# The softmax coefficient of a differential attention from two per-row scalars, with one inversion of the first sums per query block

## The chip, the cores and the metric

The kernel runs on one core of one Trainium2 chip. The metric is the device time in microseconds (us), from runs of the whole program; lower is better. The engines are named as in the profile: PE (matmul), PEld (PE's weight loads), DVE (vector), ACT (activation), POOL (the general vector engine), SP (the queue that issues DMAs).

## What is computed

The input is 8 sequences of 1024 rows of 512 numbers. Each row is normalised and projected to 32 query heads, 16 key heads and 8 value heads, the first two with rotary positions. Two neighbouring query heads make one output head, so there are 16 output heads. What matters here, cut from the reference:

```python
scores = jnp.einsum('bhqd,bhkd->bhqk', q, k)           # causal, 32 heads
probs = jax.nn.softmax(scores + causal, axis=-1)
probs = probs.reshape(bsz, H, 2, tgt_len, tgt_len)     # H = 16
diff = probs[:, :, 0] - lambda_full * probs[:, :, 1]
attn = jnp.einsum('bhqk,bhkd->bhqd', diff, v)
var = jnp.mean(attn ** 2, axis=-1, keepdims=True)
attn = attn * rsqrt(var + EPS) * subln_weight * (1 - LAMBDA_INIT)
out = attn @ Wo.T
```

Then follow the residual sum, a second normalisation, a feed-forward layer with ternary weights (512 to 2048 to 512, GELU) and a second residual sum.

## The kernel before

**Tiles and blocks.** A sequence is cut into 8 query blocks of 128 rows. Block t attends to 128 x (t + 1) keys, so its score rows are 128 to 1024 wide. The 8 blocks of sequence 0 are written out once, the 8 blocks of sequences 1 to 7 are the body of a loop, and three more blocks empty the pipeline. There are 64 blocks with 16 output heads each: 1024 heads in all.

**Steps of a block.** Each engine has its own program, written out by hand over 32 half steps (`hs`), two for a head. The order on an engine is fixed; semaphores tie the engines together. For one head:

1. PE writes two score tiles to PSUM (L832, and the mask by L833).
2. DVE takes the negated row maxima, `NM` (L665, one of two instructions, for blocks 4 to 7; L673, one instruction for both, for blocks 0 to 3).
3. ACT takes the exponentials, E1 and E2 (L541). Its accumulator writes the two row sums to `SUM[:, block parity, 0 or 1, head column]`.
4. DVE, in `diff`: the reciprocal of both sums into `RS` (L684, two elements a row), then `CC = SUM0 * neglam * (1 / SUM1)` (L686, one element a row), then `E1 = E2 * CC + E1` (L689, the full width). With SUM0 = first sum, E1 is then the difference of the two softmaxes times SUM0. `neglam` is minus the reference's `lambda_full`, one value for each row.
5. PE transposes E1 (L844), ACT copies the result out of PSUM (L553), and PE multiplies it with V (L867).

**The rest of a block.** The missing factor 1 / SUM0 is applied to all 16 heads at once, a block later at half step 6 (`AT_ROWS`, L727), from `RS[:, block parity, 0, :]`. The constant `SUM_INVERSE` (half step 5) stands in the schedule and is used by no line of the kernel before. Around the heads, DVE also does the normalisation (L623 to L631), the rotary products (L646 to L648), the remainders of split numbers (L660), the mean squares (L732, L735), and the sums with the residual (L738, L755). POOL does `x ** -0.5` (L437, L484), sums and splits (L442 to L449), the split of the hidden layer in three instructions (L458, L460, L462, in odd blocks only), and parts of the block's end (L481, L488, L500).

**Waits within `diff`.** L686 waits on semaphore `d_chain` for L684, and L689 waits on it for L686. L684 waits for both exponentials.

Of the kernel before, what the change touches and what calls it, by code (L numbers as in the profile page):

```python
# [32 lines left out]
F32 = mybir.dt.float32  # L33
# [3 lines left out]
ALU = mybir.AluOpType  # L37
# [3 lines left out]
P = 128  # L41
B, S, D = 8, 1024, 512
H, KVH = 16, 8
# [136 lines left out]
def diff_attention_ffn(nc, x, wqT, wkT, wvT, woT, lams, subw, w1T, b1, w2T, b2, rope, out):  # L180
    ctx = ExitStack()
    with ctx:
        def sb(name, shape, dt):
            return ctx.enter_context(nc.sbuf_tensor(name, shape, dt))

        def sem(name):
            return ctx.enter_context(nc.semaphore(name))
# [27 lines left out]
        DT = sb("DT", [P, TILES, HALF, P], F32)  # L215
        NM = sb("NM", [P, 8], F32)
        SUM = sb("SUM", [P, 2, 2, H], F32)
        RS = sb("RS", [P, 2, 2, H], F32)
        CC = sb("CC", [P, 2], F32)

        VST = sb("VST", [P, DKV], F32)
# [70 lines left out]
        max_ready = sem("max_ready")  # L292
        exp_done = sem("exp_done")
        d_chain = sem("d_chain")
        d_ready = sem("d_ready")
        t_ready = sem("t_ready")
        dt_ready = sem("dt_ready")
# [43 lines left out]
        def after(eng, signal, value):  # L341

            if not isinstance(value, int) or value > 0:
                eng.wait_ge(signal, value)
# [268 lines left out]
        def _(dve):  # L613
# [62 lines left out]
            def diff(b, i, n):  # L676

                u = i * H + n
                gu = b * N_U + u
                w = P * (i + 1)  # L680
                e = 512 * (u % 2) if i < 4 else 0
                col = 8 * (n // 8) + 4 * (n % 2) + (n % 8) // 2
                after(dve, exp_done, 2 * gu + 2)
                nc.vector.reciprocal(RS[:, i % 2, :, col], SUM[:, i % 2, :, col]).then_inc(d_chain, 1)  # L684
                after(dve, d_chain, 2 * gu + 1)
                nc.vector.scalar_tensor_tensor(out=CC[:, u % 2:u % 2 + 1], in0=SUM[:, i % 2, 0, col:col + 1], scalar=neglam[:, 0:1],  # L686
                                               in1=RS[:, i % 2, 1, col:col + 1], op0=ALU.mult, op1=ALU.mult).then_inc(d_chain, 1)
                after(dve, d_chain, 2 * gu + 2)
                nc.vector.scalar_tensor_tensor(out=E1[:, u % 2, 0:w], in0=E2[:, e:e + w], scalar=CC[:, u % 2:u % 2 + 1],  # L689
                                               in1=E1[:, u % 2, 0:w], op0=ALU.mult, op1=ALU.add).then_inc(d_ready, 1)  # L690

            def dve_work(T):
                b, t, nb, nf = T.b, T.t, T.nb, T.nf
                for hs in range(HS_TILE):
                    s, h = divmod(hs, 2)
                    if T.attend:
                        if t >= 4:
                            row_max(b, t, s, h)
                        elif h == 0:
                            row_max_pair(b, t, s)  # L700
                    if h == 0 and T.before(s - 1):
                        diff(*T.before(s - 1))
                    if T.attend:
                        slot = X[:, (t + 1) % 4, :]
                        if hs == LN1_STATS:

                            after(dve, x_in[(t + 1) % 2], 16 * (b * (TILES // 2) + (t + 1) // 2) + 16)
                            variance(0, slot, nb)
                        if hs == LN1_ROWS:
                            after(dve, m_x2t, nf)  # L710
                            normalise(0, slot, nb, xn_ready)
                        if hs == Q_ROPE:
                            rope_mul(nb, T.next, 0)
                        if hs == KV_ROPE:
                            rope_mul(nb, T.next, 1, b + 1)
                        if hs == Q_REST:
                            rest(nb, 0)
                        if hs == K_REST:
                            rest(nb, 1)
                    if T.finish:  # L720
                        tok = TOK[:, :].rearrange("p (c d) -> p c d", d=DV)
                        x1 = X1[:, (t - 1) % 4, :]
                        if hs == AT_ROWS:
                            after(dve, m_at, nf + 1)
                            if T.attend:
                                after(dve, m_xt, nb + 1)
                            nc.vector.tensor_tensor(tok, M[:, :].rearrange("p (c d) -> p c d", d=DV),  # L727
                                                    RS[:, (t - 1) % 2, 0, :].unsqueeze(2).broadcast_to([P, H, DV]),
                                                    ALU.mult).then_inc(attn_ready, 1)
                        if hs == MEAN_SQ:  # L730
                            after(dve, sq_ready, nf + 1)
                            nc.vector.tensor_reduce(MS[:, :], SQ[:, :].rearrange("p (c d) -> p c d", d=DV), AX.X,  # L732
                                                    ALU.add).then_inc(ms_chain, 1)
                            after(dve, ms_chain, nf + 1)
                            nc.vector.tensor_scalar(VE[:, :], MS[:, :], 1.0 / DV, EPS, ALU.mult, ALU.add).then_inc(ms_ready, 1)  # L735
                        if hs == O_SUM:
                            after(dve, m_wo, nf + 1)
                            nc.vector.tensor_tensor(x1, M[:, :], X[:, (t - 1) % 4, :], ALU.add).then_inc(x1_ready, 1)  # L738
                        if hs == LN2_STATS:
                            after(dve, x1_ready, nf + 1)  # L740
                            variance(1, x1, nf)
                        if hs == LN2_ROWS:
                            after(dve, m_ant, nf + 1)
                            normalise(1, x1, nf, xn2_ready)
                        if hs == LN2_REST:
                            after(dve, x2h_ready, nf + 1)
                            c = slice(P * ((t - 1) % 2), P * ((t - 1) % 2) + P)
                            nc.vector.scalar_tensor_tensor(
                                out=X2L[:, :, c], in0=M[:, :].rearrange("p (k n) -> p k n", k=KD), scalar=XS,
                                in1=X2H[:, :, c], op0=ALU.mult, op1=ALU.subtract).then_inc(x2_ready, 1)  # L750
                    if T.w2 and hs in OUT_AT:
                        j = OUT_AT.index(hs)
                        after(dve, f2_ready, T.no + j + 1)
                        after(dve, o_out, 16 * (T.no + j))
                        nc.vector.scalar_tensor_tensor(out=OUT[:, :], in0=F[:, :], scalar=1.0 / HS,  # L755
                                                       in1=X1[:, (t + j) % 4, :], op0=ALU.mult,
                                                       op1=ALU.add).then_inc(o_sum, 1)
# [277 lines left out]
```

## Time and profile before

| | |
|---|---|
| Time, median of 3 runs | 4437.56 us |
| Lowest and highest of the 3 | 4431.58 and 4438.31 us |
| Span of the profiled execution | 4427.3 us |
| The profiled execution's own time | not recorded; the median is 10.3 us above its span |
| Busy: PE, DVE, ACT, POOL | 81%, 78%, 66%, 33% of the span |
| Granted PE clock, mean of the core | 0.903 of full speed |

The span goes from the first to the last instruction of one execution; what lies around it is start and end of the program. Busy time of an engine is the union of its instructions' times. The idle time before an instruction is put down to what released it last.

### The profile page before, as it was taken

To read this page: it belongs to the slowest core of one execution; us is meant where nothing else is said; L and a number is where in the kernel's file an instruction comes from. 1 tells how busy PE (TensorE), PEld (TensorE's weight loads), DVE (VectorE), ACT (ScalarE), POOL (GpSimd) and SP (SyncE) were. 2 spreads that over 40 slices of the span, in tenths; PEclk is the share of its full clock that TensorE was granted. 3 is DMA by queue.
4 is the path that set the end of the run, shared out by engine and by line. 5 is a ranking of instruction groups with operands and counts; after the bars stand their busy time and mean duration, and the time that the engine had idled before them with its cause. 6 is when DMAs were issued, how large, how long until landed. Compare 5 with 4: busy or idle time off the path is not lost.

```text
span 4427.3 us, 80970 instructions
## 1 busy us (share of the span) xinstructions
PE 3604.6 (81%) x23454; PEld 2143.3 (48%) x23454; DVE 3467.0 (78%) x6124; ACT 2909.6 (66%) x6786; POOL 1450.2 (33%) x1563
## 2 busy tenths in 40 slices
PE   2688888888788887888878988888878888888886
PEld 1345544455444554544544544455544555444553
DVE  6778877888678886788867887678877788678891
ACT  1567756677566775667756766567666677567772
POOL 0233233332333333323343323433133332333323
PEclk7789989999899899998899988999989899899898
DMA  4212112211122112112122120222112121222110
GB/s 131 51 24 43 24 43 43 38 24 30 38 43 43 22 34 48 37 32 38 25 43 43 30 37 20 44 41 43 24 41 43 24 40 24 43 43 41 21 37 14
DMA packets 146768, 166.71 MB, mean 38 GB/s; under 512 B 16640, under 2 KB 117632, under 8 KB 145792
## 3 DMA queue, kind: packets, MB, share of 16 engines
q1 hardware_dynamic: 146304, 161.13, 18.0%
q8 instruction: 218, 3.57, 0.4%
q14 instruction: 246, 2.02, 0.2%
HBM read 105.95 MB, written 55.12 MB: 36 GB/s over the span
## 4 chain that ended last, share of the span: by engine, by line
PE 35%; DVE 28%; issue 22%; ACT 8%; DMA 3%; SPq 2%; POOL 2%; DVEq 1%; ACTq 0%; POOLq 0%
DVE NM L665 10%; PE M L867 6%; PE M L817 6%; PE F L889 5%; PE SP_ L832 5%; PE DP L844 5%; DVE E L689 4%; DVE CC L686 3%; PE F L902 3%; ACT E L541 2%; DMA KST<-scratch 2%; PE M L811 2%; ACT L541 2%; DVE RS L684 1%; DVE NM L673 1%
## 5 line engine op out<-in xcount | busy, mean ns | idle before, releaser
L541 ACT ACTIVATE E<-SP_,NM 128x256 f32<-128x256 f32 (+7 forms) x2048 | 1518.6, 743 | 733.6 <-DVE NM L665 526.4
L665 DVE TENSOR_REDUCE NM<-SP_ 128x1 f32<-128x896 f32 (+3 forms) x1024 | 1032.6, 1017 | 225.1 <-PE SP_ L833 222.9
L832 PE MATMUL SP_<-KST,QST 96*128 96x512 bf16 (+3 forms) x3072 | 864.1, 355 | 407.7 <-ACT E L541 345.5
L689 DVE SCALAR_TENSOR_TENSOR E<-E,CC 128x512 f32<-128x512 f32 (+7 forms) x1024 | 994.6, 971 | 36.1
L553 ACT ACTIVATE DT<-DP 128x512 f32<-128x512 f32 (+3 forms) x1024 | 527.8, 515 | 546.2 <-PE DP L844 524.0
L844 PE MATMUL DP<-ident,E 128*128 128x128 f32 x3328 | 614.5, 302 | 208.6 <-DVE E L689 207.3
L673 DVE TENSOR_REDUCE NM<-SP_ 128x2 f32<-128x1024 f32 (+3 forms) x512 | 419.8, 820 | 297.2 <-PE SP_ L833 290.3
L832 PEld LDWEIGHTS SP_<-KST,QST 96*128 96x128 bf16 x3072 | 278.7, 103 | 762.7 <-ACT E L541 537.1
L844 PEld LDWEIGHTS DP<-ident,E 128*128 128x128 f32 x3328 | 391.1, 153 | 382.2 <-issue 203.1
L889 PE MATMUL F<-X2H,W1Q 128*128 128x256 f16 x2048 | 502.0, 283 | 69.9 <-ACT HP L596 65.8
L817 PE MATMUL M<-WQKV,WT 128*128 128x512 f32 x1040 | 530.8, 607 | 8.4 <-DVE T L648 4.1
L889 PE MATMUL F<-X2L,W1Q 128*128 128x256 f16 x2048 | 501.1, 283 | 0.0
L833 PE MATMUL SP_<-maskb,identb 128*128 128x128 bf16 x2048 | 460.9, 234 | 0.0
L902 PE MATMUL F<-W2Q,HH 128*128 128x512 fp8e4 x1024 | 394.6, 385 | 33.1 <-DVE SQ L755 18.7
L541 ACT ACTIVATION_READ_ACCUMULATOR E<-SP_,NM 128x1 f32 x2048 | 414.3, 202 | 0.0
L902 PE MATMUL F<-W2Q,HL 128*128 128x512 fp8e4 x1024 | 393.0, 384 | 0.0
L686 DVE SCALAR_TENSOR_TENSOR CC<-SUM,neglam,RS 128x1 f32<-128x1 f32 x1024 | 317.9, 310 | 36.4
L458 POOL TENSOR_SCALAR HH<-HP 128x512 f16<-128x512 f32 x256 | 170.4, 666 | 529.9 <-ACT HP L602 513.7
L867 PE MATMUL M<-DT,V 128*32 128x256 f32 x4608 | 326.8, 422 | 0.1
L833 PEld LDWEIGHTS SP_<-maskb,identb 128*128 128x128 bf16 x2048 | 215.5, 105 | 192.1 <-issue 64.2
L462 POOL TENSOR_TENSOR HL<-HP,HH 128x512 f16<-128x512 f32 x256 | 297.9, 1164 | 21.3
L889 PEld LDWEIGHTS F<-X2H,W1Q 128*128 128x128 fp8e4 x2048 | 207.7, 101 | 171.9 <-issue 145.9
(86 smaller groups left out, 4780.3 us busy)
## 6 DMA issues: line engine op xcount, KB each, us to landing
QST<-scratch SPq DMA_DIRECT2D x390, 128.0 KB, 4.4
scratch<-SPL SPq DMA_DIRECT2D x65, 576.0 KB, 2.8
KST<-scratch SPq DMA_DIRECT2D x390, 64.0 KB, 5.0
X<-in_x SPq DMA_DIRECT2D x66, 256.0 KB, 3.1
out<-SQ SPq DMA_DIRECT2D x64, 256.0 KB, 2.1
KST<-in_w1T SPq DMA_DIRECT2D x1, 4096.0 KB, 19.2
DT<-in_w2T SPq DMA_DIRECT2D x1, 4096.0 KB, 28.7
WQKV<-in_wqT SPq DMA_DIRECT2D x1, 1024.0 KB, 7.3
```

Of the source, the lines that this page charges most:

```text
L541: act.activation(dst, score_out(i, 2 * n + k, w), ACT.Exp, bias=NM[:, (2 * u + k) % 8:(2 * u + k) % 8 + 1], scale=1.0, accum_out=SUM[:, i ...
L553: act.activation(DT[:, k0:k1, n % HALF, :], (DP, DX)[g][:, 0:P * (k1 - k0)].rearrange("p (k q) -> p k q", q=P), ACT.Copy).then_inc(dt_read ...
L665: nc.vector.tensor_reduce(NM[:, m:m + 1], score_out(i, 2 * n + k, P * (i + 1)), AX.X, ALU.max, negate=True).then_inc(max_ready, 1)
L673: nc.vector.tensor_reduce(NM[:, m:m + 2], SP_[:, k:k + 2, 0:P * (i + 1)], AX.X, ALU.max, negate=True).then_inc(max_ready, 2)
L689: nc.vector.scalar_tensor_tensor(out=E1[:, u % 2, 0:w], in0=E2[:, e:e + w], scalar=CC[:, u % 2:u % 2 + 1], in1=E1[:, u % 2, 0:w], op0=ALU. ...
L817: ins = pe.matmul(M[:, :], WT[:, P * j:P * (j + 1)], w[:, j, c0:c0 + 512], start=(j == 0), stop=(j == KD - 1))
L832: pe.matmul(SP_[:, k[a // 512], 0:n], q, KST[0:ROWS, a // P:(a + n) // P, kk, :], start=True, stop=not last)
L833: ins = pe.matmul(SP_[:, k[(w - P) // 512], (w - P) % 512:(w - P) % 512 + P], identb[:, :], maskb[:, :], start=False, stop=True)
L844: ins = pe.transpose((DP, DX)[g][:, P * (k % 4):P * (k % 4 + 1)], E1[:, u % 2, P * k:P * (k + 1)], ident[:, :])
L867: ins = pe.matmul(M[DV * q:DV * (q + 1), 0:2 * P], V[:, k, v:v + DV], DT[:, k, 2 * q:2 * q + 2, :], start=(k == 0), stop=(k == i), skip_gr ...
L889: ins = pe.matmul(F[:, 2 * P * j:2 * P * (j + 1)], W1Q[:, c, P * f:P * (f + 1)], xp[:, c, :], start=(c == 0 and xp is X2H), stop=(c == KD ...
L902: ins = pe.matmul(F[:, :], hp[:, f, P * j:P * (j + 1)], W2Q[:, f, :], start=(f == 0 and hp is HH), stop=(f == FT - 1 and hp is HL))
```

## The change

Three things are done. The reciprocal of a head takes the second sum alone, into a new tile `R2` of two columns (one for each head parity). The coefficient CC is made by a `tensor_scalar` with one tensor input (R2) and two scalar operands that are read per row from SBUF (the first sum and `neglam`), in place of a `scalar_tensor_tensor` with two tensor inputs (SUM and RS) and one such scalar. And the first sums of a block are inverted by one new reciprocal of 16 elements a row at half step 5 of the next block, into an `RS` that has one copy in place of two; L727's counterpart waits for it on a new semaphore, `inv_ready`.

```diff
-        RS = sb("RS", [P, 2, 2, H], F32)
+        R2 = sb("R2", [P, 2], F32)
+        RS = sb("RS", [P, H], F32)
...
                 after(dve, exp_done, 2 * gu + 2)
-                nc.vector.reciprocal(RS[:, i % 2, :, col], SUM[:, i % 2, :, col]).then_inc(d_chain, 1)
+                nc.vector.reciprocal(R2[:, u % 2:u % 2 + 1], SUM[:, i % 2, 1, col:col + 1]).then_inc(d_chain, 1)
                 after(dve, d_chain, 2 * gu + 1)
-                nc.vector.scalar_tensor_tensor(out=CC[:, u % 2:u % 2 + 1], in0=SUM[:, i % 2, 0, col:col + 1], scalar=neglam[:, 0:1],
-                                               in1=RS[:, i % 2, 1, col:col + 1], op0=ALU.mult, op1=ALU.mult).then_inc(d_chain, 1)
+                nc.vector.tensor_scalar(CC[:, u % 2:u % 2 + 1], R2[:, u % 2:u % 2 + 1], SUM[:, i % 2, 0, col:col + 1],
+                                        neglam[:, 0:1], ALU.mult, ALU.mult).then_inc(d_chain, 1)
...
+                        if hs == SUM_INVERSE:
+                            nc.vector.reciprocal(RS[:, :], SUM[:, (t - 1) % 2, 0, :]).then_inc(inv_ready, 1)
                         if hs == AT_ROWS:
+                            after(dve, inv_ready, nf + 1)
                             after(dve, m_at, nf + 1)
                             if T.attend:
                                 after(dve, m_xt, nb + 1)
                             nc.vector.tensor_tensor(tok, M[:, :].rearrange("p (c d) -> p c d", d=DV),
-                                                    RS[:, (t - 1) % 2, 0, :].unsqueeze(2).broadcast_to([P, H, DV]),
+                                                    RS[:, :].unsqueeze(2).broadcast_to([P, H, DV]),
                                                     ALU.mult).then_inc(attn_ready, 1)
```

DVE's instructions at half steps 4 to 6 of block 1, before (L673 to L689 are one head's; NM are the row maxima, E stands for E1 and E2, M is a PSUM tile):

```order
L631 TENSOR_SCALAR TOK<-X,MV,RST 128x512 [waits ln1_rstd]
L673 TENSOR_REDUCE NM<-SP_ 128x2 [waits s_ready]
L684 RECIPROCAL RS<-SUM 128x2 [waits exp_done]
L686 SCALAR_TENSOR_TENSOR CC<-SUM,neglam,RS 128x1 [waits d_chain]
L689 SCALAR_TENSOR_TENSOR E<-E,CC 128x256 [waits d_chain]
L673 TENSOR_REDUCE NM<-SP_ 128x2 [waits s_ready]
L684 RECIPROCAL RS<-SUM 128x2 [waits exp_done]
L686 SCALAR_TENSOR_TENSOR CC<-SUM,neglam,RS 128x1 [waits d_chain]
L689 SCALAR_TENSOR_TENSOR E<-E,CC 128x256 [waits d_chain]
L727 TENSOR_TENSOR TOK<-M,RS 128x512 [waits m_xt,m_at]
```

The same place in the changed program, where R is the new tile R2 and the line numbers are those of the changed kernel:

```order
L633 TENSOR_SCALAR TOK<-X,MV,RST 128x512 [waits ln1_rstd]
L675 TENSOR_REDUCE NM<-SP_ 128x2 [waits s_ready]
L686 RECIPROCAL R<-SUM 128x1 [waits exp_done]
L688 TENSOR_SCALAR CC<-R,SUM,neglam 128x1 [waits d_chain]
L691 SCALAR_TENSOR_TENSOR E<-E,CC 128x256 [waits d_chain]
L726 RECIPROCAL RS<-SUM 128x16
L675 TENSOR_REDUCE NM<-SP_ 128x2 [waits s_ready]
L686 RECIPROCAL R<-SUM 128x1 [waits exp_done]
L688 TENSOR_SCALAR CC<-R,SUM,neglam 128x1 [waits d_chain]
L691 SCALAR_TENSOR_TENSOR E<-E,CC 128x256 [waits d_chain]
L732 TENSOR_TENSOR TOK<-M,RS 128x512 [waits m_xt,m_at,inv_ready]
```

A head has as many DVE instructions as before, in the same places and with the same waits. One row is new in a block: the reciprocal of 16 elements, one head ahead of the instruction that reads it.

## Rows read from the trace of the kernel before

**Rows 1.** The page: busy shares, then the chain that ended last, by engine.
```profile
PE 3604.6 (81%) x23454; PEld 2143.3 (48%) x23454; DVE 3467.0 (78%) x6124; ACT 2909.6 (66%) x6786; POOL 1450.2 (33%) x1563
...
PE 35%; DVE 28%; issue 22%; ACT 8%; DMA 3%; SPq 2%; POOL 2%; DVEq 1%; ACTq 0%; POOLq 0%
```

**Rows 2.** Stages of one sequence (blocks 2, 5 and 7): each engine's busy time.
```profile
core 0: us, PE busy (x) PEld busy (x) DVE busy (x) ACT busy (x) POOL busy (x), PEclk, DMA share, GB/s
...
2314.90:2367.80 52.90, 46.34 (x275) 25.51 (x268) 42.30 (x89) 30.39 (x88) 13.42 (x13) 0.98 0.25 49
...
2495.90:2572.60 76.70, 64.28 (x443) 41.29 (x440) 63.17 (x103) 61.17 (x126) 33.04 (x35) 0.89 0.15 27
...
2648.60:2738.70 90.10, 72.19 (x510) 46.55 (x509) 75.80 (x101) 69.20 (x125) 31.46 (x35) 0.88 0.12 25
```

**Rows 3.** The chain over the whole span, summed by line.
```profile
by line: issue 21.5%; DVE NM L665 10.1%; PE M L867 6.4%; PE M L817 6.3%; PE F L889 5.4%; PE SP_ L832 5.1%; PE DP L844 4.8%; DVE E L689 4.1%; DVE CC L686 3.4%; PE F L902 3.3%; ACT E L541 2.5%; DMA KST<-scratch 2.0%; PE M L811 1.6%; ACT L541 
```

**Rows 4.** Groups of DVE by line: busy us, mean ns; idle before.
```profile
L686 DVE SCALAR_TENSOR_TENSOR CC<-SUM,neglam,RS 128x1 f32<-128x1 f32 x1024 | 317.9, 310 | 36.4
...
L784 DVE TENSOR_SCALAR HP<-KST,thr 128x2048 f32<-128x2048 f32 x4 | 5.1, 1286 | 0.1
...
L761 DVE TENSOR_SCALAR WQKV<-WQKV 128x2048 f32<-128x2048 f32 x1 | 1.2, 1227 | 13.4 <-DMA ropet<-in_rope 13.4
```

**Rows 5.** Single lines of DVE: duration in ns, least/median/longest, first and last start.
```profile
L686 DVE SCALAR_TENSOR_TENSOR CC<-SUM,neglam,RS x1024: 218/219/1102, 89.4 to 4333.3; 128x1 f32<-128x1 f32 x171
...
L684 DVE RECIPROCAL RS<-SUM x1024: 148/157/171, 89.2 to 4333.1; 128x2 f32<-128x2 f32 x171
...
L627 DVE TENSOR_SCALAR VE<-MV x129: 153/154/155, 15.6 to 4359.1; 128x1 f32<-128x1 f32 x129
...
L631 DVE TENSOR_SCALAR TOK<-X,MV,RST x129: 530/541/945, 16.5 to 4360.0; 128x512 f32<-128x512 f32 x129
...
L735 DVE TENSOR_SCALAR VE<-MS x64: 174/174/176, 141.8 to 4345.4; 128x16 f32<-128x16 f32 x64
...
L732 DVE TENSOR_REDUCE MS<-SQ x64: 673/677/685, 141.1 to 4344.6; 128x16 f32<-128x512 f32 x64
```

**Rows 6.** The instructions in order of time: POOL and DVE in block 5.
```profile
2553.86 0.62 POOL L458 TENSOR_SCALAR HH<-HP 128x512 f16<-128x512 f32 x1 [11.00 <-ACT HP L602]
2554.07 0.15 DVE L627 TENSOR_SCALAR VE<-MV 128x1 f32<-128x1 f32 x1
...
2557.83 0.16 DVE L684 RECIPROCAL RS<-SUM 128x2 f32<-128x2 f32 x1
2557.92 0.62 POOL L460 TENSOR_SCALAR HP<-HP 128x512 f32<-128x512 f32 x1 [0.19 <-POOL HH L458]
2558.02 0.52 DVE L686 SCALAR_TENSOR_TENSOR CC<-SUM,neglam,RS 128x1 f32<-128x1 f32 x1
2558.58 2.01 DVE L689 SCALAR_TENSOR_TENSOR E<-E,CC 128x768 f32<-128x768 f32 x1
2558.63 1.15 POOL L462 TENSOR_TENSOR HL<-HP,HH 128x512 f16<-128x512 f32 x1
```

**Rows 7.** The same view: first and last of 122 coefficients longer than 0.521 us.
```profile
101.88 0.93 DVE L686 SCALAR_TENSOR_TENSOR CC<-SUM,neglam,RS 128x1 f32<-128x1 f32 x1
...
4322.16 1.08 DVE L686 SCALAR_TENSOR_TENSOR CC<-SUM,neglam,RS 128x1 f32<-128x1 f32 x1
4323.27 1.72 DVE L689 SCALAR_TENSOR_TENSOR E<-E,CC 128x1024 f32<-128x1024 f32 x1
```

**Rows 8.** L689: the page's group, its durations (ns), and two undisturbed ones.
```profile
L689 DVE SCALAR_TENSOR_TENSOR E<-E,CC 128x512 f32<-128x512 f32 (+7 forms) x1024 | 994.6, 971 | 36.1
...
L689 DVE SCALAR_TENSOR_TENSOR E<-E,CC x1024: 350/885/2286, 89.6 to 4333.5; 128x256 f32<-128x256 f32 x22, 128x640 f32<-128x640 f32 x22, 128x1024 f32<-128x1024 f32 x22, 128x128 f32<-128x128 f32 x21
...
2005.29 1.02 DVE L689 SCALAR_TENSOR_TENSOR E<-E,CC 128x768 f32<-128x768 f32 x1
...
2648.88 1.28 DVE L689 SCALAR_TENSOR_TENSOR E<-E,CC 128x1024 f32<-128x1024 f32 x1
```

More of the change, by code:

```diff
@@ L294, in diff_attention_ffn @@
         d_chain = sem("d_chain")
+        inv_ready = sem("inv_ready")
         d_ready = sem("d_ready")
```

## The prediction

> **What bounds the kernel now.** I read the page first. PE is busy for 81% of the span and DVE for 78%; on the chain of work that ended last PE has 35%, DVE 28% and issue 22% [rows 1]. So no engine is the bound alone. By stages, a late block (5 or 7) has DVE busy for 63.2 of 76.7 and 75.8 of 90.1 us, while an early one (2) has 42.3 of 52.9 us [rows 2]. DVE has the least room in the late blocks, where PE waits for it as much as it for PE. Then the chain by line: the coefficient L686 holds 3.4% of 4427.3, which is 150 us [rows 3], out of the 317.9 us that it is busy at all [rows 4]. That is 0.47, and I take it as the share of time on this spot of DVE that the span feels.
>
> **What L686 costs, and why it is uneven.** Its mean is 310 ns [rows 4], its median 219, its longest 1102 [rows 5], for one element a row. If all took 219 ns they would make 224 us; the other 94 us is something else. The instructions in order of time show it [rows 6]: at 2558.02 the coefficient starts while POOL's L460 runs (2557.92 to 2558.54), and it ends as L460 ends, after 0.52 us. L689 starts at 2558.58, POOL's L462 at 2558.63, and L689 takes 2.01 us where the same width takes 1.02 undisturbed [rows 8]. One head has waited for POOL twice, once in each instruction that has two tensor inputs in SBUF. L684, with one input, never takes over 171 ns, and L627, a `tensor_scalar` of one element, takes 153 to 155 in all 129 cases [rows 5], also where it starts inside L458 [rows 6]. L631, a `tensor_scalar` of 512 elements, does reach 945 against a median of 541 [rows 5].
>
> Counted over all rows, 269 coefficients are longer than 225 ns, and 122 of them longer than 521 ns [rows 7]; those 122 hold 70 of the 94 us.
>
> **The changed coefficient, undisturbed.** The trace has no `tensor_scalar` of one element with two scalars read from SBUF. I build it. One without such scalars: 154 ns (L627) [rows 5]. One scalar costs 59 ns: L784, with one, takes 1286 ns for 2048 elements, L761, with none, 1227 [rows 4]. Two cost about 119: L761 gives (1227 - 154) / 2048 = 0.524 ns an element, so 512 elements make 268, and L631's 541 less 268 less 154 leaves 119 [rows 4, 5]. So 154 + 119 = 273 ns, 54 more than 219. Over 1024 heads this is **+55 us of DVE**. Bounds: 154 ns if the scalars' reading is hidden (-67 us), 273 from above, as both ways to price a scalar agree.
>
> **The reciprocals.** One element in place of two: the least and longest of L684 are 148 and 171 for two [rows 5], one element at the measured 0.524 ns is lost in that, so 0 (from -9 us, if all took 148, to 0). The block's new one, 16 elements, is not in the trace; the nearest row of 16 elements is L735 with 174 ns, the far bound L732, which reads 512 elements, with 677 [rows 5]. I take 174, since L684 lies so near to L627: 64 x 0.174 = **+11 us of DVE** (11 to 43). Behind it on DVE stand the row maximum and a whole head before L727's counterpart asks for it, over a microsecond of work, so `inv_ready` costs nothing, except in the one closing block, where its cover is gone and it costs at most that 0.2 us. No DMA and nothing on the queues of SP and POOL moves.
>
> Costs together: 66 us of DVE, times 0.47, **+31 us** on the span.
>
> **What the wait is worth.** My choice is that the new coefficient, having one tensor input and one element, does not wait, like L627. L689 still does. It would start 273 + 35 ns after the coefficient's start (35 is 36.4 us over 1024, the idle time before L686 [rows 4]; the same before L689 by its 36.1 [rows 8]). A wait shorter than 308 ns is then gone; of a longer one 308 ns is. That is 24 us for the 147 short ones and 122 x 0.308 = 38 us for the long, together 62.
>
> The second wait goes as well, where there was a first. L689 undisturbed takes 350 ns for 128 columns and 1.28 us for 1024 [rows 8], about 817 on the mean of the eight widths, 836 us in all; it is busy 994.6 [rows 8], so 158 us of it are waits. In the head of rows 6, L689 would wait at 2558.33 already, take over at 2558.54 when L460 ends, ahead of L462, and be through at 2559.56 in place of 2560.59. Counted over all rows, 62 of the 158 us stand right behind one of the 122 long coefficients, as the 1.72 at 4323.27 against 1.28 [rows 7, 8]; these I take as gone. Behind a shorter wait, 78 heads have a second one; there POOL's next instruction begins one coefficient (219 ns) earlier, which gives back 17 us. Together 62 + 62 + 17 = **141 us of DVE**.
>
> A saving on one path counts only until the next path is longest; a cost counts in full. PE, within 10% of DVE's load in every stage of rows 2, is that next path. So I weigh the saving with a third instead of 0.47: **-47 us**.
>
> The Trainium skill, page "SBUF — State Buffer", section "Who interferes with whom", has DVE and GpSimd share a port pair as an exclusive lock, taken by DVE instructions with two SBUF inputs and by those in a two-port mode, and it lists `tensor_scalar` among those that can enter such a mode. By the first half the coefficient stops waiting; by the second it could go on, and then the sum would be +31 instead of -16. For L631 the trace agrees with the second half (541 to 945 ns), for the one element of L627 it does not (153 to 155).
>
> **The sum.** Against the profiled execution: 4427.3 + 31 - 47 = 4411.3 us of span. What lies around it is 10.3 us, so 4421.6; against the median of the runs, 4437.56 - 16 = **4422 us**.
>
> **Rivals.**
>
> *A, the forecast: the first wait is gone and the second with it.* 4422 us, own range 4403 to 4440 (the saving weighed by 0.47: -66 + 31 = -35; by 0.2: -28 + 31 = +3). For it: L627 and L684 never wait, and each instruction of POOL in rows 6 is followed by a gap in which a waiting DVE can take over. Chance 0.5.
>
> *B, the wait is handed on.* L689 waits for what L686 waited for, and afterwards still collides with POOL's next instruction, as POOL, no longer held up by the coefficient, has that one ready sooner. Then only the 62 us go, a third of which is 21: 4437.56 + 31 - 21 = 4448. For it: POOL's three instructions follow each other within 0.2 us. Against: L686 itself was let in between two of them. Chance 0.2.
>
> *C, slower: the coefficient goes on waiting.* Reading the two scalars, or the instruction's mode, needs what POOL holds. Then nothing is gained: 4437.56 + 31 = 4469. For it: no row shows a small `tensor_scalar` with scalars from SBUF beside a busy POOL, and L631 waits. Against: L627. It decides if less than 93 of the 141 us of DVE come back, since 93 / 3 = 31. Chance 0.12.
>
> *D, much faster.* The scalars' reading is hidden (no 55 us), and the whole 141 us count by 0.47: -66 + 5 = -61, so 4377. Against: L784 and L631 show the price openly. Chance 0.08.
>
> *E, it does nothing that can be told.* Cost and saving both vanish in the waits for PE, of which DVE has many in blocks 0 to 3: 4437. Chance 0.1.
>
> **How the numbers follow.** The forecast is A's, 4422. A and B with their surroundings, E, and most of C are held by 4392 to 4466; below it lies D, above it a part of C, 2 in 10 with the tails. 0.2% of the time is 9 us, about what a measurement of this kernel can tell from no change. Faster than 4428.7: 0.35 from A, 0.08 from D, 0.02 from B and E, 0.45. Within: 0.13 of A, 0.08 of B, 0.08 of E, 0.01 of C, 0.30. Slower: 0.10 of B, 0.11 of C, the rest from the edges of A and E, 0.25.
>
> **What the changed kernel's profile would show.** The coefficient has a median near 273 ns and hardly a longer one, its busy time falls from 318 to about 280 us; a longest far above 300 ns would be C. L689's busy time falls from 995 us towards 950 (less 62 and 17, more the 32 us of long waits that it meets itself); under B it grows, by those 32 us. The block's reciprocal takes near 174 ns, 64 times; an amount per element of tens of ns would show there. The odd blocks, with 31 to 33 us of POOL's work, become shorter; the even ones, with 13 us in block 2 [rows 2], gain less and may be longer by at most 16 x 0.054 + 0.174 = 1.0 us each. The forecast is wrong if the two scalars cost more than 119 ns in a one-element instruction, if POOL wins the gap before L689, or if the blocks turn out to be set by PE, so that 141 us less of DVE's waits leave the span where it is.

## The result

The changed kernel takes 4372.64 us (median of 4 runs, 4370.70 to 4373.63), the kernel before 4437.94 us beside it. The ratio is 0.9853, 95% interval 0.9840 to 0.9867: 65 us, or 1.5%, faster. The forecast was 4422 us and its range ended at 4392, so the direction was right and the size too small by a factor of four.

The page of the changed kernel, busy shares and the chain, to stand beside [rows 1]:

```profile
PE 3625.1 (83%) x23454; PEld 2157.1 (49%) x23454; DVE 3369.0 (77%) x6188; ACT 2913.5 (67%) x6786; POOL 1495.9 (34%) x1563
...
PE 41%; DVE 25%; issue 19%; ACT 8%; DMA 3%; SPq 2%; POOL 1%; DVEq 1%; ACTq 1%; POOLq 0%
```

DVE is busy 98 us less (3467.0 to 3369.0), POOL 46 us more (1450.2 to 1495.9), and the span is 58.4 us shorter (4427.3 to 4368.9). These are numbers of one execution of each kernel. Every execution whose span is on record took 1.7 to 1.9 us longer than its span, so the profiled one of the kernel before took an estimated 4429.1 us. It was 8 us faster than the median, and the 10.3 us in the table ahead of the prediction are not start and end of the program. On the chain DVE has gone from 28% to 25%, PE from 35% to 41%. The same three blocks of the same sequence as in [rows 2]:

```profile
2275.80:2328.30 52.50, 46.59 (x271) 25.57 (x262) 41.88 (x89) 30.46 (x88) 13.76 (x14) 0.96 0.23 50
2456.50:2531.60 75.10, 63.64 (x452) 41.34 (x450) 61.94 (x103) 60.89 (x125) 33.54 (x35) 0.91 0.16 28
2609.70:2697.90 88.20, 72.85 (x507) 46.56 (x506) 71.26 (x102) 69.05 (x125) 34.07 (x35) 0.87 0.11 25
```

Against [rows 2] block 2 is 0.4 us shorter, block 5 is 1.6 us shorter and block 7 1.9 us. On the mean over the loop's sequences all odd blocks are shorter (by 0.8, 2.1, 1.3 and 1.9 us), but so is block 0, by 2.3 us, and block 6 is 2.0 us longer (76.1 to 78.1).

Now the lines that were changed, in groups (busy us, mean ns; idle before). Line numbers are 2 to 5 higher than before.

```profile
L688 DVE TENSOR_SCALAR CC<-R,SUM,neglam 128x1 f32<-128x1 f32 x1024 | 279.5, 273 | 37.3
...
L691 DVE SCALAR_TENSOR_TENSOR E<-E,CC 128x512 f32<-128x512 f32 (+7 forms) x1024 | 928.6, 907 | 36.2
...
L686 DVE RECIPROCAL R<-SUM 128x1 f32<-128x1 f32 x1024 | 158.7, 155 | 65.7 <-ACT E L543 61.1
...
L633 DVE TENSOR_SCALAR TOK<-X,MV,RST 128x512 f32<-128x512 f32 x129 | 74.3, 576 | 2.5 <-POOL RST L439 1.5
...
L726 DVE RECIPROCAL RS<-SUM 128x16 f32<-128x16 f32 x64 | 15.7, 245 | 0.0
```

and the coefficient's spread, least, median and longest:

```profile
L688 DVE TENSOR_SCALAR CC<-R,SUM,neglam x1024: 272/273/276, 89.4 to 4274.7; 128x1 f32<-128x1 f32 x171
```

No coefficient waits any more: 276 ns is the longest of 1024, where it was 1102 [rows 5]. Among them are 295 that start while a wide instruction of POOL (256 or 512 elements a row) has over 220 ns to run. Its undisturbed time is the 273 ns that the prediction had built from four other rows. The row sum (L689 before, L691 now) is busy 928.6 us in place of 994.6 [rows 8].

The head of [rows 6], in the same block of the same sequence:

```profile
2518.62 0.15 DVE L686 RECIPROCAL R<-SUM 128x1 f32<-128x1 f32 x1
2518.70 0.62 POOL L462 TENSOR_SCALAR HP<-HP 128x512 f32<-128x512 f32 x1 [0.19 <-POOL HH L460]
...
2518.81 0.27 DVE L688 TENSOR_SCALAR CC<-R,SUM,neglam 128x1 f32<-128x1 f32 x1
...
2519.12 1.02 DVE L691 SCALAR_TENSOR_TENSOR E<-E,CC 128x768 f32<-128x768 f32 x1
...
2519.41 1.74 POOL L464 TENSOR_TENSOR HL<-HP,HH 128x512 f16<-128x512 f32 x1
```

Before, the coefficient took 0.52 us and the row sum 2.01; now they take 0.27 and 1.02. From the reciprocal's start to the row sum's end it was 2.76 us and is 1.52. POOL's L464, 1.15 us long when undisturbed, takes 1.74: the row sum now comes first, and POOL waits for DVE instead of DVE for POOL. By line, POOL's additional busy time is 28 us in the first instruction of this split (L458 before, 170.4 us, now 198.2), 18 in its third (297.9, now 315.7) and 7 and 6 in two others, less 15 in its second (195.4, now 180.1).

The second wait can be counted. Before, 95 row sums start 10 to 47 ns ahead of an instruction of POOL and still wait for it, 62 us in all; that of [rows 6], 47 ns ahead, is one. In the changed kernel 3 do, 1.8 us. Row sums that start 49 to 200 ns ahead of POOL, 23 before and 10 now, do not wait.

### The profile page after: what moved, and what is told of

Its sections match the earlier page's. It is cut to its first block, busy times and chain, and to the rows that moved or that the text cites. A ratio compares the mean times of both kernels' runs of the same rounds, so it can differ in the third digit from the quotient of the medians.

```text
span 4368.9 us, 81035 instructions
## 1 busy us (share of the span) xinstructions
PE 3625.1 (83%) x23454; PEld 2157.1 (49%) x23454; DVE 3369.0 (77%) x6188; ACT 2913.5 (67%) x6786; POOL 1495.9 (34%) x1563
## 4 chain that ended last, share of the span: by engine, by line
PE 41%; DVE 25%; issue 19%; ACT 8%; DMA 3%; SPq 2%; POOL 1%; DVEq 1%; ACTq 1%; POOLq 0%
DVE NM L667 9%; PE M L822 7%; PE M L872 7%; PE SP_ L837 6%; PE F L894 6%; PE DP L849 5%; PE F L907 4%; DVE E L691 3%; ACT E L543 3%; DVE CC L688 2%; DMA KST<-scratch 2%; PE M L816 2%; DVE NM L675 2%; PE SP_ L838 1%; PE DX L849 1%
## 5 line engine op out<-in xcount | busy, mean ns | idle before, releaser
L691 DVE SCALAR_TENSOR_TENSOR E<-E,CC 128x512 f32<-128x512 f32 (+7 forms) x1024 | 928.6, 907 | 36.2
L894 PE MATMUL F<-X2H,W1Q 128*128 128x256 f16 x2048 | 512.1, 287 | 71.0 <-ACT HP L598 67.0
L894 PE MATMUL F<-X2L,W1Q 128*128 128x256 f16 x2048 | 510.7, 286 | 0.0
L460 POOL TENSOR_SCALAR HH<-HP 128x512 f16<-128x512 f32 x256 | 198.2, 774 | 519.9 <-ACT HP L604 503.7
L872 PE MATMUL M<-DT,V 128*32 128x256 f32 x4608 | 342.8, 439 | 0.1
L464 POOL TENSOR_TENSOR HL<-HP,HH 128x512 f16<-128x512 f32 x256 | 315.7, 1233 | 21.3
L688 DVE TENSOR_SCALAR CC<-R,SUM,neglam 128x1 f32<-128x1 f32 x1024 | 279.5, 273 | 37.3
```

The costliest lines, as they stand in the source:

```text
L872: ins = pe.matmul(M[DV * q:DV * (q + 1), 0:2 * P], V[:, k, v:v + DV], DT[:, k, 2 * q:2 * q + 2, :], start=(k == 0), stop=(k == i), skip_gr ...
L894: ins = pe.matmul(F[:, 2 * P * j:2 * P * (j + 1)], W1Q[:, c, P * f:P * (f + 1)], xp[:, c, :], start=(c == 0 and xp is X2H), stop=(c == KD ...
```

## The experiments

Each was timed beside the kernel before on the same chip, 4 to 11 runs each. To compare them with each other, their ratios to the kernel before are used, and 0.001 is 4.4 us. "Above the changed kernel" is the ratio less 0.9853, times 4438; with intervals of about 0.0013 on either side of each ratio, such a difference is known to within some 8 us. DVE's busy time is that of one profiled execution. The two theories at the start: that DVE's time counts by about 0.6 wherever it lies (58.4 / 98), against a rival by which other parts of the edit or other weights had their share.

**The coefficient's form alone.** Both sums are inverted in each head as before.

```diff
-                nc.vector.scalar_tensor_tensor(out=CC[:, u % 2:u % 2 + 1], in0=SUM[:, i % 2, 0, col:col + 1], scalar=neglam[:, 0:1],
-                                               in1=RS[:, i % 2, 1, col:col + 1], op0=ALU.mult, op1=ALU.mult).then_inc(d_chain, 1)
+                nc.vector.tensor_scalar(CC[:, u % 2:u % 2 + 1], RS[:, i % 2, 1, col:col + 1], SUM[:, i % 2, 0, col:col + 1],
+                                        neglam[:, 0:1], ALU.mult, ALU.mult).then_inc(d_chain, 1)
```

> The coefficient's new form alone; both sums are inverted per head as before and there is no block inversion. Theory 1 (all of the gain is the coefficient's wait, and DVE time counts by about 0.6 wherever it is): as the changed kernel without its 15.7 us of block inversion and with 4 us more of reciprocals, so 12 x 0.6 = 7 us below it: 4366 us. Rival (the block inversion and the shorter reciprocals brought part of it): above the changed kernel, 4380 us or more. In both the coefficient takes 273 ns and never waits.

Measured: 0.9856 (0.9841 to 0.9871), 4377.81 us. The whole gain is there without the block inversion. The time itself lies between the two that were expected, but the ratio is the changed kernel's. Of the 12 us of DVE to be saved against the changed kernel 8 are there (3361.1 against 3369.0 us), and they brought nothing that shows. The coefficient (279.4 us) and the row sum (927.7) are as short as in the changed kernel.

**The inversions alone.** The coefficient keeps two inputs.

```diff
+                nc.vector.scalar_tensor_tensor(out=CC[:, u % 2:u % 2 + 1], in0=SUM[:, i % 2, 0, col:col + 1], scalar=neglam[:, 0:1],
+                                               in1=R2[:, u % 2:u % 2 + 1], op0=ALU.mult, op1=ALU.mult).then_inc(d_chain, 1)
-                nc.vector.tensor_scalar(CC[:, u % 2:u % 2 + 1], R2[:, u % 2:u % 2 + 1], SUM[:, i % 2, 0, col:col + 1],
-                                        neglam[:, 0:1], ALU.mult, ALU.mult).then_inc(d_chain, 1)
```

> The block inversion and the one-element reciprocals alone; the coefficient keeps the two-input form. Theory 1: 12 us more of DVE than before, 7 us slower: 4445 us; the coefficient's mean stays near 310 ns. Rival (the inversion brought part of the gain): under 4430 us.

Measured: 0.9997 (0.9988 to 1.0006), 4437.63 us. They neither help nor cost; the 7 us of cost that theory 1 expected lie just outside the interval. The coefficient, with one-element reciprocals and all, waits as before, and the row sum behind it too:

```profile
L691 DVE SCALAR_TENSOR_TENSOR E<-E,CC 128x512 f32<-128x512 f32 (+7 forms) x1024 | 998.1, 975 | 36.1
...
L688 DVE SCALAR_TENSOR_TENSOR CC<-SUM,neglam,R 128x1 f32<-128x1 f32 x1024 | 316.8, 309 | 36.3
```

So the 38 us less in the coefficient and the 66 us less in the row sum both hang on the one changed instruction.

**One more instruction with one input in every head** of the changed kernel, which prices evenly spread DVE time.

```diff
                 after(dve, exp_done, 2 * gu + 2)
+                nc.vector.tensor_scalar(DUM[:, u % 2:u % 2 + 1], SUM[:, i % 2, 1, col:col + 1], 1.0, 0.0, ALU.mult, ALU.add)
                 nc.vector.reciprocal(R2[:, u % 2:u % 2 + 1], SUM[:, i % 2, 1, col:col + 1]).then_inc(d_chain, 1)
```

> The changed kernel with one more DVE instruction a head in front of the reciprocal: a tensor_scalar of one element with one input and constants, into a tile that nothing reads, with nothing waiting for it. Two such instructions without a wait between them start 70 ns apart in the setup (85.05 and 85.12 us), so it costs 72 us of DVE if it behaves so, 158 us if it holds the next one for its full 154 ns. Theory 1 (DVE time in a head counts by 0.6): 72 x 0.6 = 43, 4416 us. Rival (a cost counts by 0.3 at most, since PE is the next bound, and only the waits behind POOL are dear): under 4394 us.

Measured: 0.9897 (0.9882 to 0.9912), 4394.49 us. DVE is busy 3428.2 us, 59 more, and the time is 20 us above the changed kernel: 0.33 for each us, with the 8 us of uncertainty 0.2 to 0.5, and so below theory 1's weight.

**The same with two inputs in SBUF.**

```diff
+                nc.vector.tensor_tensor(DUM[:, u % 2:u % 2 + 1], SUM[:, i % 2, 0, col:col + 1], SUM[:, i % 2, 1, col:col + 1], ALU.mult)
```

> As the run with one more one-input instruction, but the extra one is a tensor_tensor of one element with two inputs in SBUF (160 ns in the trace of before, against 154). Its difference to that run is the price of waiting for POOL once more in a head, at no other change. Theory 1: 94 us of waits in the extra instruction and up to 66 us more in the row sum behind it, by 0.6: 55 to 95 us above the one-input run. Rival (the wait is handed on, the row sum would have waited anyway): within 15 us of the one-input run.

Measured: 1.0038 (1.0026 to 1.0051), 4455.31 us, 0.0141 or 63 us above the run with one input. The two instructions side by side, first the one with one input, then the one with two, and that one's least, median and longest duration:

```profile
L687 DVE TENSOR_SCALAR DUM<-SUM 128x1 f32<-128x1 f32 x1024 | 149.0, 145 | 67.7 <-ACT E L544 64.1
```
```profile
L687 DVE TENSOR_TENSOR DUM<-SUM 128x1 f32<-128x1 f32 x1024 | 280.2, 274 | 68.9 <-ACT E L544 66.0
```
```profile
L687 DVE TENSOR_TENSOR DUM<-SUM x1024: 142/158/1112, 88.4 to 4340.1; 128x1 f32<-128x1 f32 x171
```

A second input in SBUF costs 131 us: 14 ns more in the median (158 against 144), 14 us of it, and the rest waits. DVE is busy 117 us more (3544.9 less 3428.2). The time went up by 63 us: 0.54 for each us. The rival, that the row sum would have waited anyway, is refuted; it is only 11 us shorter (918.5 against 929.5 us). So waits look dearer than evenly spread work, though 0.54 and 0.33 are apart by hardly more than their uncertainty. Three theories for that were put on record: their place (P), their size in one head (S), or something of the waits themselves (L).

**A delay of one input in the 34 heads of a sequence that had waited before, and in 34 quiet ones.**

```diff
+AT_HEADS = {0: (3, 5, 7, 8, 10), 1: (3, 5, 7, 11, 13, 14, 15), 2: (5, 8), 3: (5, 7, 8, 9, 14, 15), 4: (5, 8, 10, 15), 5: (5, 8, 13), 6: (5, 8, 10), 7: (7, 8, 9, 13)}
...
+                if n in AT_HEADS[i]:
+                    nc.vector.tensor_reduce(DUM[:, u % 2:u % 2 + 1], ropet[:, :, :, :].rearrange("p a b c -> p (a b c)"), AX.X, ALU.max)
                 nc.vector.reciprocal(R2[:, u % 2:u % 2 + 1], SUM[:, i % 2, 1, col:col + 1]).then_inc(d_chain, 1)
```

> The changed kernel with one more DVE instruction, in 34 of the 128 heads of a sequence (272 in all): a maximum over 256 numbers of a table, one input, into a tile that nothing reads, in front of the reciprocal. The 34 are the heads whose coefficient waited for POOL in the trace of before. Such an instruction takes about 0.41 us and never waits for POOL, about 0.33 us from start to start, so some 90 us of DVE in all. Theory P (waits behind POOL are dear because of the heads in which they lie, where DVE holds up the span): it counts by 0.5 or more, 45 us above the changed kernel, 4418 us or more. Theory S (they are dear because each is large, and a small delay is taken up by slack): the same as the delay at quiet heads. Theory L (the waits themselves are special, as by what POOL loses; DVE time counts by 0.34 in every form): 31 us, 4403 us, in both.

> The same instruction as often in each block, but in 34 heads whose coefficient did not wait in the trace of before. Theory P: it counts by 0.34 or less, under 4403 us, and at least 15 us below the run with the delay at the waiting heads. Theory S: by 0.5, 4418 us, as that run. Theory L: 4403 us, as that run.

Measured: 0.9981 (0.9972 to 0.9990), 4430.05 us, at the heads that had waited, 57 us above the changed kernel; 0.9945 (0.9932 to 0.9959), 4415.31 us, at the quiet ones, 41 us above. DVE is busy 96 and 76 us more: 0.59 and 0.54. Theory L falls: DVE time of a kind that never waits for POOL is as dear as the waits when it comes in lumps. The place makes 16 us of difference, and 20 us of DVE busy time go with it, from row sums that wait more (942.6 against 919.7 us). Part of the 16 us may be the clock: PE's mean granted clock was 0.901 of full speed in the median run at the heads that had waited and 0.905 in that at the quiet ones.

**The form by head.** The two-scalar form only in the 34 heads, two inputs in the other 94.

```diff
+                if n in TWO_SCALARS[i]:
+                    nc.vector.tensor_scalar(CC[:, u % 2:u % 2 + 1], R2[:, u % 2:u % 2 + 1], SUM[:, i % 2, 0, col:col + 1],
+                                            neglam[:, 0:1], ALU.mult, ALU.mult).then_inc(d_chain, 1)
+                else:
+                    nc.vector.scalar_tensor_tensor(out=CC[:, u % 2:u % 2 + 1], in0=SUM[:, i % 2, 0, col:col + 1], scalar=neglam[:, 0:1],
+                                                   in1=R2[:, u % 2:u % 2 + 1], op0=ALU.mult, op1=ALU.mult).then_inc(d_chain, 1)
```

> The changed kernel, but the coefficient takes the two-scalar form only in those 34 heads of a sequence; the other 94 take the two-input form of before (219 ns in place of 273) with the one-element reciprocal. 752 x 54 ns = 41 us less of DVE. If uniform DVE time counts by 0.34 and the quiet heads stay quiet: 14 us below the changed kernel, 4359 us. If POOL's instructions move onto other heads, so that the two-input form waits in them: 4373 us or more.

Measured: 0.9864 (0.9848 to 0.9879), 4376.08 us, no better than the changed kernel. POOL's instructions did move onto heads that had been quiet: the two-input coefficient takes 238 ns on its mean in place of 219, and the row sum 918 against 907.

```profile
L695 DVE SCALAR_TENSOR_TENSOR CC<-SUM,neglam,R 128x1 f32<-128x1 f32 x752 | 178.8, 238 | 26.6
...
L692 DVE TENSOR_SCALAR CC<-R,SUM,neglam 128x1 f32<-128x1 f32 x272 | 74.2, 273 | 9.9
```

Of 41 us that were to be saved DVE kept 13.

**Two extra instructions with one input in every head.**

```diff
+                nc.vector.tensor_scalar(DUM[:, u % 2:u % 2 + 1], SUM[:, i % 2, 1, col:col + 1], 1.0, 0.0, ALU.mult, ALU.add)
+                nc.vector.tensor_scalar(DUM[:, 2 + u % 2:3 + u % 2], SUM[:, i % 2, 1, col:col + 1], 1.0, 0.0, ALU.mult, ALU.add)
```

> As the run with one more one-element instruction of one input per head, but with two of them: about 2 x 63 = 126 us more of DVE than the changed kernel, in equal parts on all heads. If its price is linear: 0.34 x 126 = 43 us, 4416 us. Theory S (small delays fall into slack, which runs out): more than twice the first one's 22 us, over 4425 us. If DVE's limit is rarely reached: under 4405 us.

Measured: 0.9996 (0.9979 to 1.0014), 4437.34 us, the median of 11 runs from 4415.29 us, at a granted clock of 0.915, to 4458.85, at 0.900. DVE is busy 137 us more and the time is 63 us above the changed kernel. The first such instruction cost 20 us, the second 44 for 78 us of DVE: 0.33, then 0.57. The price looks not linear, as theory S has it, though the second's extra cost, 24 us, has an uncertainty of some 16, but a price by the sum over all heads (theory C, put on record for the next two runs) would explain this too.

**The delay at half its size**, a maximum over 128 numbers, at quiet heads and at those that had waited.

```diff
-                    nc.vector.tensor_reduce(DUM[:, u % 2:u % 2 + 1], ropet[:, :, :, :].rearrange("p a b c -> p (a b c)"), AX.X, ALU.max)
+                    nc.vector.tensor_reduce(DUM[:, u % 2:u % 2 + 1], ropet[:, 0, :, :].rearrange("p b c -> p (b c)"), AX.X, ALU.max)
```

> The delay at the 34 quiet heads, but a maximum over 128 numbers in place of 256: about 0.20 us from start to start, 272 times, 54 us of DVE, which is less than the 65 us that one extra one-element instruction in every head adds (that cost 22 us). Theory S (a delay counts by its size in one head, as small ones fall into slack): 0.48 x 54 = 26 us above the changed kernel, 4399 us. Theory C (it counts by the sum over all heads; the first 65 us are cheap and the next dear, as the full delay of 90 us and the two extra instructions of 129 us suggest): 18 us or less, 4391 us or less.

> The same half delay at the 34 heads whose coefficient waited for POOL before: 54 us of DVE and, as in the full delay, some more waits of the row sum behind it. Theory C with the place counting too: 0.64 against 0.48 in the full delay, so a third more than at the quiet heads: 24 to 35 us above the changed kernel, 4397 to 4408 us. If the place counts only through size: as the quiet run within 5 us.

Measured: 0.9931 (0.9917 to 0.9945) and 0.9930 (0.9917 to 0.9944), 35 and 34 us above the changed kernel. The sum over the heads is less than that of the one extra instruction in each (DVE busy +54 and +43 us against +59), and the price is more (35 and 34 us against 20). The 15 us between the half delay at quiet heads and the one extra instruction have an uncertainty of 9. That speaks against theory C, which allowed 18 us at the quiet heads, and for S: a delay counts by how large it is in one head. The second run alone decides nothing, as C with the place counting too had said 24 to 35 us. A rival was not tested: the lumps also lie unevenly among the blocks, 7 heads in block 1 and 2 in block 2, and are made by another instruction. The place made no difference at this size. What may take up the small delays can be read in the idle time of the row maxima, in the changed kernel, with one extra instruction in each head, and with the half delay at quiet heads:

```profile
L667 DVE TENSOR_REDUCE NM<-SP_ 128x1 f32<-128x896 f32 (+3 forms) x1024 | 1034.2, 1018 | 257.8 <-PE SP_ L838 254.0
```
```profile
L668 DVE TENSOR_REDUCE NM<-SP_ 128x1 f32<-128x896 f32 (+3 forms) x1024 | 1032.6, 1018 | 226.2 <-PE SP_ L840 223.0
```
```profile
L671 DVE TENSOR_REDUCE NM<-SP_ 128x1 f32<-128x896 f32 (+3 forms) x1024 | 1032.9, 1017 | 244.2 <-PE SP_ L844 241.1
```

The 59 us that are spread evenly take 32 us out of DVE's idle time before the row maxima of blocks 4 to 7; the 54 us in lumps take 14. This is read from one execution of each. By these executions' own times alone (4370.70, 4398.84 and 4403.96 us) the weights are 0.48 and 0.62, and so nearer to each other than by the medians.

**The extra instruction on the kernel before.**

> The kernel before with the extra one-element instruction of one input in every head: 65 us more of DVE above where it stood, in the same form as the run on the changed kernel. If the price grows with DVE's load: 0.5 to 0.66 of 65, so 32 to 43 us above before, 4470 to 4481 us. If it levels off, as the changed kernel with two extra instructions (4437 us at 3506 us of DVE) suggests: under 4458 us.

Measured: 1.0067 (1.0054 to 1.0081), 30 us above before, for 65 us of DVE: 0.46. Neither branch was met cleanly; nothing shows that the price levels off.

**No reciprocal in the heads.**

```diff
-                nc.vector.reciprocal(R2[:, u % 2:u % 2 + 1], SUM[:, i % 2, 1, col:col + 1]).then_inc(d_chain, 1)
-                after(dve, d_chain, 2 * gu + 1)
-                nc.vector.tensor_scalar(CC[:, u % 2:u % 2 + 1], R2[:, u % 2:u % 2 + 1], SUM[:, i % 2, 0, col:col + 1],
+                nc.vector.tensor_scalar(CC[:, u % 2:u % 2 + 1], SUM[:, i % 2, 1, col:col + 1], SUM[:, i % 2, 0, col:col + 1],
...
-                after(dve, d_chain, 2 * gu + 2)
+                after(dve, d_chain, gu + 1)
```

> The changed kernel without the reciprocal of each head: the coefficient multiplies the second sum in place of its inverse, so the output is not the reference's. 158 us less of DVE busy, about 190 us less of its time. If PE is the bound by now (the version by head and the form alone, both with less DVE time than the changed kernel, were not faster): above 4355 us. If DVE time still counts by 0.34 or more: 65 us less or more, 4308 us or below.

Measured: 0.9675 (0.9661 to 0.9688), 4289.23 us, 79 us below the changed kernel, for 161 us less of DVE busy: 0.49. DVE is not off the path in the changed kernel; PE is not yet the bound alone. The granted clock was 0.919 against 0.900, and how much of the 79 us goes with it is not shown by this run.

| Run | DVE busy, us, against | time, us, against | per us | median granted clock | at one clock: time, us (per us), estimate |
|---|---|---|---|---|---|
| one input more, each head | +59, changed | +20, changed | 0.33 | 0.902 | +26 (0.44) |
| the second such | +78, the first | +44, the first | 0.57 | 0.908 | +56 (0.72) |
| half delay, 34 quiet / waiting heads | +54 / +43, changed | +35 / +34, changed | 0.64 / 0.80 | 0.905 / 0.906 | +37 (0.69) / +41 (0.96) |
| delay, 34 quiet / waiting heads | +76 / +96, changed | +41 / +57, changed | 0.54 / 0.59 | 0.905 / 0.901 | +54 (0.71) / +60 (0.62) |
| two inputs in place of one | +117, one input | +63, one input | 0.54 | 0.902 | +58 (0.50) |
| one input more, each head | +65, before | +30, before | 0.46 | 0.902 | +24 (0.37) |
| no reciprocal | -161, changed | -79, changed | 0.49 | 0.919 | -43 (0.27) |
| the change itself | -98, before | -65, before | 0.67 | 0.900 | -67 (0.68) |

The last two columns look at a rival: that the granted clock, and not DVE's time, made some of the differences. The change itself did not profit from it (0.900, and 0.901 to 0.903 in the runs of the kernel before). Among runs of one and the same kernel a clock higher by 0.001 goes with 2.2 us less, over 126 runs; the estimate brings all to 0.901 with that number. Why a kernel gets more clock or less is not shown. Evenly spread time stays the cheaper at one clock, but the waits (0.50) come near to it, and the difference by place shrinks to 6 us. Whether the clock is the cause of these differences or goes along with them is not shown either.

## Why the prediction was wrong in size

**The coefficient undisturbed: right.** 273 ns from the rows of other instructions, 273 measured (272 to 276), +55 us over the heads. So each scalar read from SBUF costs about 59 ns in an instruction of one element as in one of 2048.

**"The new coefficient does not wait, like L627": right.** Rival C, by which it goes on waiting, is refuted by its longest of 276 ns. That the Trainium skill, page "SBUF — State Buffer", section "Who interferes with whom", lists `tensor_scalar` among the instructions that can contend when their operands meet its conditions, did not come to bear on one element: 295 coefficients ran beside a reading POOL and none took over 276 ns.

**The reciprocals: nearly right.** One element saves 3.6 us (forecast 0, from -9), the block's one takes 245 ns and not 174, 15.7 us in place of 11. With 155 ns for one element, 159 for two and 245 for sixteen it costs about 6 ns an element, which L735, taken as its row, could not show. On the time it does not matter (0.9856 without, 0.9853 with it).

**The wait's worth on DVE: mis-sized, too small.** The forecast had 141 us back: 62 of first waits, net of what L691 would meet itself, and 79 of second ones. Measured are 94 us in the coefficient and 66 in the row sum, 160 together, and 4.5 us more in L633, a third kind of instruction that waits for POOL (78.8 to 74.3 us). What L691 would meet itself was about right: in the changed kernel 112 row sums wait for the rest of the instruction of POOL that ran when their coefficient started, 28 us in all, where the forecast had 32. Too small were the second waits: of 158 us of waits in the row sum 92 are left, 28 of the first kind and 64 others, so 94 us of second waits are gone and not 79. The forecast's example misread its head: the coefficient there had waited 0.30 us and then run its own 0.22, so by the forecast's own rule of 308 ns nothing was left for L689, and it would not have waited until 2558.54. In the changed kernel L691 starts 0.42 us into the same instruction of POOL (0.62 us long), and neither takes any longer than alone (1.02 and 0.62 us).

**"I weigh the saving with a third instead of 0.47": this is the step that failed.** It rested on the thought that a cost on one path counts in full and a saving only until the next path is the longest. The runs show the weights the other way round. Costs were even, 54 ns in every head; such DVE time counts by 0.33 above the changed kernel and 0.46 above the kernel before (0.44 and 0.37 at one clock), not more than the 0.47 that was taken. Savings were lumps, 0.35 us on the mean in 269 coefficients (94 / 269) and two thirds of a us in 231 row sums (158 / 231, counted as those more than 15 ns above the least of their width); lumps of 0.2 to 0.3 us count by 0.54 to 0.8, waits of an added instruction by 0.54. Put in: the costs, 55 + 16 - 4 = 67 us, by 0.33 are 22; for 65 us of gain the 164 us of waits have to count by (65 + 22) / 164 = 0.53, which is what the run with a second input gives. Even if the costs were free it would be 65 / 164 = 0.40, so a third is too small whatever they count. With the forecast's own 66 and 141 us these weights make 22 - 75 = -53 us, so of the 49 us by which the forecast was short, 37 are the weights and the rest is the 23 us of waits more that went (19 in the row sum, 4.5 in L633). The weight of 0.53 is fitted to the measured gain and not measured for the change by itself.

**The share of 0.47** was taken from the chain, where a long wait and a short instruction are added up alike; that 150 us of 318 was a mean over the two kinds is argued, not shown. With 0.47 on both sides and the forecast's own amounts the sum would have been 31 - 66 = -35 us.

**Rivals.** B, the wait handed on, is refuted as the whole story: under it the row sum grows, and it fell by 66 us. The 28 us above are handed on, and A had them too. D gave 4377 us and so came nearest, but by luck: its gross saving, 141 us by 0.47, is 66 us and so nearly the net gain, but it leaves out the scalars' 55 us of cost, which are there, and takes 141 us for waits of 164. E, nothing that can be told, is out.

**The blocks: half right.** In the sequence shown, odd ones became shorter as said (block 5 by 1.6, block 7 by 1.9 us), and block 2, expected to gain less or be longer by at most 1.0, is 0.4 us shorter. Over the loop's sequences the odd ones hold, but block 0 gained 2.3 us, more than any odd block, and block 6 became 2.0 us longer. The runs do not show why.

What stays open: whether it is slack before the row maxima alone that takes up small delays, or PE's and ACT's too (only DVE's idle time was read for it), and why the full delay at quiet heads counts a little less than the half one (0.54 and 0.64, within the runs' intervals). The cause of the weights stays open in part: the gain hangs on the removed waits, which is shown, but that waits count by more because they come in lumps rests on differences of 15 to 25 us, hardly above their uncertainty.

## What to carry to other kernels

Where DVE and POOL work side by side, look for small DVE instructions whose longest duration is far above their median, and rewrite them with one tensor input and scalars: 54 ns more a piece bought back waits of up to 0.9 us, in the instruction and in the one behind it. Weigh time by how it comes: here 60 ns added in every head counted by 0.3 to 0.5, and nearly the same sum, added in lumps of 0.2 us or more, by 0.5 to 0.9. And a wait that is removed moves the order at the next contended place too; here it put DVE ahead of POOL, which could afford it. Before you compare two kernels to within 1%, look at the granted clock of their runs: here one kernel's time went from 4415 to 4459 us with it.

## What the hardware showed that was not expected

A DVE instruction with two inputs in SBUF pays less than the rest of POOL's instruction. Before, coefficients that started 55, 99, 170 and 305 ns into L460 (620 ns long) took 349, 304, 235 and 98 ns longer than 219. The two numbers add up to 402 to 407 each time, and those that started 572 ns or later into it took no longer. With L462 (1153 to 1157 ns) the sum is near 950: 85 ns into it 863, 620 ns into it 329, 1020 ns into it none. This is not a fraction of POOL's instruction but a fixed remainder. The wait ends 202 to 209 ns before the end of POOL's instruction if that has two inputs, whatever its kind (0.67 to 1.27 us long), and 214 to 218 ns before it if it has one.

Whether POOL lets go early, or DVE's instruction spends its first part on what POOL does not hold, the run with two inputs in SBUF helps to tell. Its extra `tensor_tensor` has no scalar and takes 158 ns in the median, and there the remainder is 138 to 146 ns for POOL's instructions with two inputs and 150 to 155 for those with one. The 62 ns between the two runs are about the 59 ns of a scalar's reading, so at least that part of a DVE instruction passes beside POOL. Told by the ends, both runs agree: a one-element instruction that waited ends 1 to 8 ns after POOL's if that has one input, 10 to 20 ns after if it has two (but for eight, before, which waited for POOL's next one as well). The start fits this too: a row sum that starts 3 to 48 ns ahead of POOL still comes second, and one that starts 49 ns ahead or more comes first.

The Trainium skill, page "SBUF — State Buffer", section "SBUF: two separate sides", has it that whichever starts first has the shared pair for the whole instruction. L691 at 2519.12 was not lengthened by L462, which ended at 2519.32, and row sums that started 10 to 47 ns ahead of POOL waited for it; so by the profile's starts and ends the rule does not hold to within some 200 ns. Counted from where DVE's first part is over it can hold, and no run here tells.
